# Deformable convolution, attention and experts on one core: absolute row distances of the tents by five ScalarE activations instead of one VectorE sum and one Abs

## What is computed

```python
offsets = conv(gn(x), offset_w) + offset_b          # (B, H, W, 9, 2): dy, dx of each tap
py = arange(H)[:, None, None] + ky + dy             # where tap k of a pixel samples
px = arange(W)[None, :, None] + kx + dx
val = bilinear(gn(x), py, px)                       # four neighbours, zero outside
out = einsum('bhwkc,kcf->bhwf', val, kernel) + bias
```

## Time and profile before

| | |
|---|---|
| median of 3 runs | 510.5 us |
| profiled execution | 507.9 us |
| its span | 506.1 us |
| mean granted TensorE clock | 0.897 of full |
| TensorE (PE) busy | 416.1 us, 82% |
| VectorE (DVE) busy | 345.3 us, 68% |
| ScalarE (ACT) busy | 289.8 us, 57% |
| GpSimd (POOL) busy | 159.5 us, 32% |
| line 582, sum over six planes, 8 times | 15.4 us |
| line 593, Abs, 8 times | 10.2 us |
| line 596, Relu, 8 times | 10.1 us |

### The profile page before, as it was taken

One profiled execution on the slowest core, in us unless ns is written; L12 is line 12 of the kernel. 1 busy time (PEld: TensorE's weight loads), 2 busy tenths in 40 slices (PEclk: granted clock), 3 DMA queues, 4 the chain that ended last, 5 costly groups with the idle time before them and its releaser, 6 DMA issues. The chain is left out here.

```text
span 506.1 us, 14009 instructions
## 1 busy us (share of the span) xinstructions
PE 416.1 (82%) x5845; PEld 307.5 (61%) x5845; DVE 345.3 (68%) x478; ACT 289.8 (57%) x531; POOL 159.5 (32%) x119
## 2 busy tenths in 40 slices
PE   1606985899999999999999999999999788227574
PEld 0204572576777677767767776767867556226274
DVE  3234668777898889889889989888896653213034
ACT  2323264778787687778677776877676456022100
POOL 2006007106534535472354446040640430310000
PEclk9756597999999999999999999999999969755589
DMA  9598969788787778588867789868730000039208
GB/s 221 97 208 189 222 144 231 179 205 177 188 205 177 177 183 186 123 207 195 186 160 174 175 176 207 198 158 198 181 71 12 2 2 12 1 70 229 84 3 166
DMA packets 33698, 75.61 MB, mean 149 GB/s; under 512 B 22365, under 2 KB 25373, under 8 KB 27293
## 3 DMA queue, kind: packets, MB, share of 16 engines
q1 hardware_dynamic: 28750, 72.68, 62.7%
q10 hardware_dynamic: 4880, 1.98, 1.7%
HBM read 64.74 MB, written 7.01 MB: 142 GB/s over the span
## 5 line engine op out<-in xcount | busy, mean ns | idle before, releaser
L1073 DVE TENSOR_TENSOR wring<-stage 96x640 f32<-96x640 f32 x192 | 173.0, 943 | 32.5 <-ACT stage L869 28.5
L1248 PE MATMUL psum<-wring,zring 96*64 96x160 f32 (+4 forms) x1728 | 124.8, 293 | 6.4 <-DVE wring L1073 6.4
L1248 PEld LDWEIGHTS psum<-wring,zring 96*64 96x64 f32 x1728 | 104.6, 141 | 20.9 <-issue 15.9
L1035 DVE TENSOR_REDUCE negmax<-psum 128x1 f32<-128x128 f32 (+3 forms) x64 | 48.3, 754 | 34.5 <-PE psum L1097 34.4
L1215 PE MATMUL psum<-kern,img 64*32 64x192 f32 x1536 | 58.5, 343 | 9.0 <-ACT zring L876 8.4
L876 ACT ACTIVATE zring<-psum 96x768 f32<-96x768 f32 x64 | 51.4, 803 | 23.0 <-PE psum L1215 21.4
L902 ACT ACTIVATE pT<-psum 128x512 f32<-128x512 f32 (+2 forms) x96 | 46.0, 483 | 28.4 <-PE psum L1105 28.1
L961 ACT ACTIVATE prob<-psum,negmax 128x128 f32<-128x128 f32 (+3 forms) x64 | 47.0, 734 | 22.9 <-DVE negmax L1035 18.4
L1093 PE MATMUL psum<-kT,qT 64*128 64x128 f32 (+4 forms) x400 | 51.7, 361 | 4.6 <-DVE kT L1030 1.5
L1105 PE MATMUL psum<-const,prob 128*128 128x128 f32 x288 | 50.5, 287 | 3.2 <-ACT pT L902 3.0
L866 ACT ACTIVATE stage<-stage,const 96x384 f32<-96x384 f32 x64 | 38.9, 608 | 20.5 <-DMA stage<-near 20.3
(11 more groups left out here) (120 smaller groups left out, 525.9 us busy)
## 6 DMA issues: line engine op xcount, KB each, us to landing
stage<-near SPq DMA_DIRECT2D x192, 288.0 KB, 5.5
w<-in_w SPq DMA_DIRECT2D x1, 2080.0 KB
tok<-in_x SPq DMA_DIRECT2D x8, 256.0 KB, 5.2
images<-img SPq DMA_DIRECT2D x8, 256.0 KB, 3.8
w<-in_w SPq DMA_DIRECT2D x1, 2048.0 KB
img<-img SPq DMA_DIRECT2D x7, 256.0 KB, 3.0
near<-tents SPq DMA_DIRECT2D x32, 45.0 KB
shifts<-offT SPq DMA_DIRECT2D x8, 128.0 KB, 6.4
```

The lines of the kernel that those rows point to most:

```text
L1035: dve.tensor_reduce(negmax[:, t:t + 1], score_rows(t, a), AX.XY, ALU.max, negate=True).then_inc(s["mx"], 1)
L1073: dve.tensor_tensor(rows[:, ky, :, place], stage[0:KX, q % STG, ky, 1:, :], stage[0:KX, q % STG, ky, 0, :].unsqueeze(1).to_broadcast([KX, ...
L1248: ins = pe.matmul(psum[C * e:C * e + C, 2 + half, (lo % 16) * W:(lo % 16 + n) * W], zring[0:KX, q % ZRING, i % 2 * 2 + e, ky * C:(ky + 1) ...
```

## The change

The sum over six planes on VectorE becomes a sum over plane 0 alone (`base`, 128 columns of the constant table). The five row planes are made by ScalarE straight from `offT`: five activations Abs(offT + bias), where the bias is a column of the new constant `rows` with the values -2 to 2. The in-place Abs goes. ScalarE therefore waits for `offT` and for the previous image's tents to be in DRAM, and no longer for VectorE; the Relu waits for all five. `leave` waits also for the previous image's five, since they read `offT`, and SyncE waits also for plane 0 before it writes the tents. The constant table shrinks from 768 to 133 columns here.

```diff
--- before.py
+++ after.py
@@ -294,13 +294,13 @@
     half = np.full((P, NT), -0.5)
     yall = ((r + 2)[:, None, None] + BR * np.arange(NT)[None, :, None] - np.arange(BR * NCH)[None, None, :]).reshape(P, -1)
 
-    kinds = np.zeros((P, KINDS, PW))
+    base = np.zeros((P, PW))
     tap = p % 32 - K * K
     for q in np.flatnonzero((tap >= 0) & (tap < K * K)):
-        kinds[q, 0] = np.arange(PW) % W + tap[q] // K - 1
-    kinds[:, 1:] = (np.arange(REACH) - REACH // 2)[None, :, None]
+        base[q] = np.arange(PW) % W + tap[q] // K - 1
+    rows = np.tile(np.arange(REACH) - REACH // 2, (P, 1))
     negx = -w[:, None].astype(np.float64)
-    parts = dict(ident=ident, same=same, diff=diff, half=half, negx=negx, kinds=kinds.reshape(P, -1), mask=mask,
+    parts = dict(ident=ident, same=same, diff=diff, half=half, negx=negx, base=base, rows=rows, mask=mask,
                  xbase=xbase, yall=yall)
     at, cols = {"early": sum(parts[n].shape[1] for n in ("ident", "same", "diff", "half"))}, 0
     for n, a in parts.items():
@@ -435,6 +435,7 @@
         to = self.near[b]
         sync.wait_ge(self.s["off_sb"], b + 1)
         sync.dma_start(self.shifts[b].rearrange("p (h q) -> p h q", h=2), self.offT[:, :, :]).then_inc(self.s_shift[b % 2], 16)
+        sync.wait_ge(self.s["t_raw"], b + 1)
         sync.wait_ge(self.s["t_ok"], b + 1)
         for j in range(4):
             place = to[2 * j:2 * j + 2].rearrange("h a n -> a h n")
@@ -568,31 +569,34 @@
         act.wait_ge(self.s["off_mm"], b + 1)
         if b > 0:
             act.wait_ge(self.s["t_raw"], b)
+            act.wait_ge(self.s["t_abs"], REACH * b)
             act.wait_ge(self.s_shift[(b - 1) % 2], 16 * ((b - 1) // 2 + 1))
             act.wait_ge(self.s["mx"], b)
         act.activation(self.offT[:, :, :], self.psum[:, 0, 0:2 * P].rearrange("p (h q) -> p h q", h=2), ACT.Identity,
                        bias=self.ob[:, 0:1]).then_inc(self.s["off_sb"], 1)
 
     def distances(self, dve, b):
-        kinds = self.cst("kinds").rearrange("p (k n) -> p k n", k=KINDS)
         if b > 0:
             for j in range(4):
                 self.tents_kept(dve, b - 1, j)
         dve.wait_ge(self.s["off_sb"], b + 1)
-        dve.tensor_tensor(self.tents[:, :, :].rearrange("p h (k n) -> p h k n", k=KINDS),
-                          self.offT[:, :, :].unsqueeze(2).to_broadcast([P, 2, KINDS, PW]),
-                          kinds.unsqueeze(1).to_broadcast([P, 2, KINDS, PW]),
-                          ALU.add).then_inc(self.s["t_raw"], 1)
+        dve.tensor_tensor(self.tents[:, :, 0:PW], self.offT[:, :, :],
+                          self.cst("base").unsqueeze(1).to_broadcast([P, 2, PW]), ALU.add).then_inc(self.s["t_raw"], 1)
         dve.tensor_reduce(self.mx[:, b:b + 1], self.offT[:, :, :], AX.XY, ALU.max,
                           apply_absolute_value=True).then_inc(self.s["mx"], 1)
 
     def tent(self, act, b, step):
         now = self.tents[:, :, PW:]
         if step == 0:
-            act.wait_ge(self.s["t_raw"], b + 1)
-            act.activation(now, now, ACT.Abs).then_inc(self.s["t_abs"], 1)
+            act.wait_ge(self.s["off_sb"], b + 1)
+            if b > 0:
+                for j in range(4):
+                    self.tents_kept(act, b - 1, j)
+            for k in range(REACH):
+                act.activation(self.tents[:, :, (k + 1) * PW:(k + 2) * PW], self.offT[:, :, :], ACT.Abs,
+                               bias=self.cst("rows")[:, k:k + 1]).then_inc(self.s["t_abs"], 1)
         else:
-            act.wait_ge(self.s["t_abs"], b + 1)
+            act.wait_ge(self.s["t_abs"], REACH * (b + 1))
             act.activation(now, now, ACT.Relu, bias=1.0, scale=-1.0).then_inc(self.s["t_ok"], 1)
```

## The result

The kernel before took 510.0 us (median of 22), the changed one 512.4 us (median of 22); the ratio is 1.0071, 95% interval 1.0046 to 1.0095. That is 3.6 us slower, between 2.3 and 4.8. The ratio and its interval are taken over the fast executions of each kernel, those within 1.5% of its own fastest (up to 512.3 us before, up to 516.4 after), while over all 22 the medians differ by 2.4 us and the means by 3.4. The profiled execution took 508.7 us, its span is 506.9, where the one of before had 507.9 and 506.1: +0.8. So the single profiles differ by less than any of these figures, and one question of this study is where the rest is.

The account below looks back on a forecast made before the run. The start was taken as bound by one serial chain of tents, the middle by TensorE with VectorE close behind. 0.78 + 0.88 + 0.3 + 0 + 0 = +2.0 us on a median of 510.5 gave 512.5, range 510.0 to 514.8.

Parts of the forecast that it names:

- Direction and place: Whole kernel: slower, chance 0.55, +2.0 us, with the cost in the start and nothing from images 3 to 7.
- The five Abs: ScalarE's tents step: about 0.50 us each, overlapping, 2.14 us until the last result; 0.88 us added ahead of the Relu.
- Rival (a): ScalarE's five Abs do not overlap: sum 3.7 us, time 514.2; chance 0.20 together with Rival (d).
- Image 0: Start, serial chain through DRAM: Abs start 0.10 us earlier, so +0.78 us, with no cushion behind.
- Image 1: Start: ScalarE has no gap between the Abs and the column tents, so +0.88 us in full.
- image 2: After the start: the Abs delay ScalarE by 0.89 us, 0.49 of slack absorbs part; about +0.3 us.
- Images 3 to 7: Middle: 0.18 us later each, absorbed by TensorE's 0.71 us wait for weights; 0, at most 0.9 us in all.
- VectorE's relief: VectorE's sum, every image: about 1.34 us freed each, falling into its own waits; worth 0.
- the table: Constant load at the start: fewer bytes could bring image rows up to 1.0 us earlier; taken as 0.
- Rival (c): Middle: VectorE is the true bound, its relief removes waits; -2.4 us, time 508.1, chance 0.10.
- (b): Start: smaller table saves 0.8 us and the Abs are cheap; about +0.1 us, time 510.6, chance 0.20.
- Rival (d): Image 1: longer idle may hold TensorE at 1.2 GHz longer; 2.0 + 1.0 us, chance 0.20 together with Rival (a).

Follow-up runs that it names:

- The moved kernels: Three kernels with image 1's Abs and Relu ahead of a ScalarE row copy, two also image 0's, against the kernel before: ratios 1.0062, 1.0056 and 1.0133.
- m_five_2to7: The changed kernel with the old scheme in images 0 and 1, five Abs only in images 2 to 7, old table size; 1.0010 of the kernel before.

## Why the prediction was right, and where not

**Direction and place: right.** Slower, 512.4 for a forecast of 512.5. That the two agree to 0.1 is luck: the base measured 0.5 lower than the one I had. The better comparison is the change, +2.0 worked out. It is 0.4 below the difference of the medians of all executions (+2.4), and 1.6 below that of the ratio (+3.6, 2.3 to 4.8), just outside its interval. So the sum was too small, by 0.4 to 1.6 us.

**The five Abs: right.** 0.503 us each and 2.09 in all, 2.12 to the Relu, for 0.50 and 2.14. Rival (a), no overlap, falls.

**Image 0: right.** +0.78 said, +0.85 at the first stage, or 0.73 without what stood in the row copy ahead; in like traces the chain carried 2.82 us for 2.82.

**Image 1 and image 2: partly.** In like traces the chain carried 3.80 for 3.70 up to image 0's tokens, so +0.88 for image 1 holds. Then some is given back: +1.04 at image 1's tokens between the two profiled executions, for 0.78 + 0.88 + 0.3 in the sum. The +0.3 of image 2 is not seen: in like traces with five Abs and with one, image 1's tokens came at 119.75 and 119.89. I had looked for cover behind each step, but not behind image 2's as a whole.

**Images 3 to 7: right.** 0 to 0.9 said; +0.47 from image 1's to image 7's tokens, 0.29 in the pair of traces. L979 came without its idle time, and the wait for the weights absorbed it, 3.3 to 2.4 as in the working.

**VectorE's relief and the table: right.** 0 each. For the relief there is 0.9999 and the pair of traces with and without VectorE's old work; the table gives 0.2 us at TensorE's first work and no gain in the time. Rival (c) falls, and (b) with both its halves: the five Abs cost their full 2.09 us, and the start is not 0.8 shorter. VectorE's waits for TensorE did not grow by as much as its work shrank: from 135 to 345 us `wring` has 4.1 more and `negmax` 0.5 less, for 5 x 1.34 = 6.7.

**The clock: the step that was mis-sized.** Rival (d) had the mechanism, a longer idle stretch and TensorE at 1.2 GHz behind it, but as a case beside the forecast, at +1.0 and with part of a 0.20. It is no case beside it: over the runs it comes on top of the chain's price, on the average by some +1 to +2 us by the counts above, through how often an execution falls in the low group. Traces show the clock lower in the start of such executions; that the later tents bring it there is argued from counts, not shown. The working read the price from one profiled execution, and the medians of this kernel's groups differ by up to 5.9 us (505.6 to 511.5) with nothing changed. The Trainium skill (TensorE: Matmul & The Clock Gate, Part 1: The HAM clock gate) says that the number of products at the low clock varies from run to run of one kernel and puts the cost of coming back to the high clock under 1% of a typical span; here the variation is there, and the groups lie up to 1.2% apart, end of the kernel included.

**The row copy: missing.** For image 1 the prediction named the tents' way through DRAM as the chain. The moved kernels show that the row copy next to it is on it too: 2.1 us of it cost 3.5.

## What to carry to other kernels

Work taken from an engine that waits for TensorE anyway was worth nothing here, and work put ahead of a serial chain on another engine counted once in full: read for each place which wait ends last, not the busy share. Where TensorE idles in a stage, price a delay there as the delay plus the half-clock time that a longer idle stretch brings, and compare single profiles only when their granted clock agrees stretch by stretch; otherwise one execution's shift hides or invents microseconds. A profile of one execution is one draw: look where its time lies among the others before reading a difference from it. Before moving a step ahead of its neighbours in an engine's list, look which engine waits for those neighbours.

## What the runs showed of the hardware

A kernel with nothing changed has groups of executions up to 5.9 us (1.2%) apart in their medians, when they are sorted by TensorE's mean granted clock; in the traces the clock differs in the start and the end.

The added ScalarE work in the middle cost more than itself: 2.05 us in each of six images gave 19.4 us instead of at most 12.3. TensorE idled 1.7 us a turn, and behind three of four such waits its granted clock fell, in 192:204 from 1.00 to 0.63 and 0.50; over a turn it was 0.90 or 0.91 for 1.00.

The granted clock of a stretch can say 1.00 while products take their half-clock time. In `m_five_2to7`, whose clock row begins with 9999, the row products between 19 and 27 us last 1.52 us, as they do at half clock, and 0.87 us at 60 us:

```profile
25.14 1.52 PE L1238 MATMUL psum<-kern,img 64*32 64x192 f32 x24 [1.63 <-ACT zring L899]
```

So a mean clock of 0.93 is not all speed: the durations of equal products decide, and the clock figure serves here to sort executions, not to explain their times.
